# The first sorted expert blocks run between the last routing steps of chunks 2 and 3

## The reference

```python
# second layer: attention of the tokens to the context, then the experts
x = x + tanh(g_xattn[1]) * attend(layernorm(x), ctx)

xt = layernorm(x)                       # 2048 x 128
logits = xt @ Wr + br                   # 8 experts
pr, idx = top_k(logits, 2)
w = softmax(pr)                         # weights of the two chosen experts
for e in range(8):                      # DFF = 512
    h = silu(xt @ W1[e] + b1[e]) * (xt @ W2[e] + b2[e])
    y = y + (h @ W3[e] + b3[e]) * cw[:, e:e+1]
x = x + tanh(g_ffn[1]) * y
```

## Time and profile before

| | us |
|---|---|
| median of 3 runs | 659.05 |
| lowest and highest run | 655.75, 662.88 |
| the profiled execution's own time | 665.03 |
| its span, first to last instruction | 663.2 |
| outside the span in that execution | 1.8 |
| router logits of chunk 3 start (line 2071) | 512.94 |
| last row scatter of chunk 3 starts (line 776) | 529.30 |
| block 0's `up` starts; block 9's `up` starts (line 2156) | 520.05; 557.42 |

### The profile page before, as it was taken

The page is one execution under the profiler, slowest core; times in us unless marked ns, Lnnn a source line. Parts: engine busy times, 40 slices in busy tenths (PEclk is TensorE's granted clock), DMA queues, the critical chain, the costliest instruction groups (busy, mean ns, idle before and its releaser), DMA issues.

```text
span 663.2 us, 9902 instructions
## 1 busy us (share of the span) xinstructions
PE 569.0 (86%) x3306; PEld 341.7 (52%) x3318; DVE 430.7 (65%) x1054; ACT 307.7 (46%) x630; POOL 205.2 (31%) x214
## 2 busy tenths in 40 slices
PE   3777898988998699899999999998845579999993
PEld 1433444444443144344444445455635479999992
DVE  4898787887377879778334857768765444444454
ACT  2554364656667562455444435455332134444441
POOL 3829201010033686001750000012562723323330
PEclk9796798999998799899999999999795679999996
DMA  7694880000059100000021001000025158999965
GB/s 273 147 191 117 139 150 3 2 2 3 1 198 349 62 0 0 1 0 0 0 77 50 1 5 9 1 0 5 29 82 179 52 168 287 330 309 322 332 211 199
DMA packets 48198, 71.14 MB, mean 107 GB/s; under 512 B 11420, under 2 KB 35300, under 8 KB 47860
## 3 DMA queue, kind: packets, MB, share of 16 engines
q1 hardware_dynamic: 45156, 65.55, 34.3%
q0 software_dynamic: 2272, 4.69, 2.0%
q10 hardware_dynamic: 720, 0.27, 0.2%
HBM read 59.12 MB, written 21.29 MB: 121 GB/s over the span
## 4 chain that ended last, share of the span: by engine, by line
PE 42%; DVE 10%; issue 4%; DMA 4%; SPq 2%; POOL 2%; ACT 1%; another core or an unknown queue 1%; POOLq 0%; DVEq 0%
PE psum L1910 18%; PE psum L2156 6%; PE psum L2167 3%; DMA wb<-in_wall_dram 3%; PE psum L1839 3%; PE psum L1841 3%; PE psum L1907 2%; DVE hidden L1268 1%; PE psum L1989 1%; SPq L591 1%; DMA back<-sorted_y 1%; POOL sorted_x L776 1%; PE psum L1908 1%; PE psum L2017 1%
## 5 line engine op out<-in xcount | busy, mean ns | idle before, releaser
L1910 PE MATMUL psum<-hidden,ew 128*128 128x512 f32 x320 | 145.5, 598 | 0.6
L853 ACT ACTIVATE probs<-psum 128x512 f32<-128x512 f32 x128 | 72.7, 597 | 59.5 <-PE psum L1698 59.0
L1910 PEld LDWEIGHTS psum<-hidden,ew 128*128 128x128 f32 x320 | 61.3, 192 | 70.8 <-issue 69.6
L1127 DVE TENSOR_REDUCE negmax<-psum 128x4 f32<-128x1024 f32 x64 | 76.9, 1218 | 20.1 <-PE psum L1675 19.9
L1605 DVE SCALAR_TENSOR_TENSOR gated<-psum,wb,silu_g 128x128 f32<-128x128 f32 x156 | 43.8, 344 | 65.4 <-ACT silu_g L1047 50.0
L2156 PE MATMUL psum<-xbT,wb 128*128 128x128 f32 x624 | 80.5, 284 | 2.8 <-DMA wb<-in_wall_dram 2.5
L2156 PEld LDWEIGHTS psum<-xbT,wb 128*128 128x128 f32 x624 | 76.6, 200 | 4.0 <-DMA wb<-in_wall_dram 3.3
L1047 ACT ACTIVATE silu_g<-psum,wb 128x128 f32<-128x128 f32 x156 | 44.6, 369 | 69.6 <-PE psum L2156 49.0
L796 POOL DMA_INDIRECT sorted_y<-yb,xb x39 | 37.3, 956 | 80.4 <-DVE yb L1597 80.4
L1698 PE MATMUL psum<-stacks 50*128 50x256 bf16 x256 | 48.4, 289 | 9.8 <-ACT probs L853 4.3
L655 POOL TENSOR_SCALAR rstd<-meanvar 128x4 f32<-128x4 f32 x16 | 4.3, 270 | 158.2 <-DVE meanvar L1065 158.1
(11 more groups left out here) (253 smaller groups left out, 987.4 us busy)
## 6 DMA issues: line engine op xcount, KB each, us to landing
wb<-in_wall_dram SPq DMA_DIRECT2D x39, 516.0 KB
wb<-in_wall_dram SPq DMA_DIRECT2D x39, 256.0 KB
sorted_x<-in_slots_dram SPq DMA_DIRECT2D x1, 9815.0 KB, 32.6
stacks<-stacked SPq DMA_DIRECT2D x12, 384.0 KB, 9.1
xb<-sorted_x SPq DMA_DIRECT2D x39, 65.0 KB
stacked<-parts SPq DMA_DIRECT2D x6, 384.0 KB, 3.4
back<-sorted_y SPq DMA_DIRECT2D x4, 512.0 KB, 7.0
stacked<-parts SPq DMA_DIRECT2D x6, 256.0 KB, 3.3
```

The costliest lines, as they stand in the source:

```text
L853: nc.scalar.activation(probs[:, g % 2, h % 4, :, :], s2[n % 2].rearrange("p (k q) -> p k q", k=2), ACT.Exp, scale=float(HD) ** -0.5).then_ ...
L1127: nc.vector.tensor_reduce(negmax[:, p].rearrange("p h q -> p (h q)"), psum[:, i:i + 2, :].rearrange("p h (q k) -> p (h q) k", q=2), AX.X, ...
L1910: last = nc.tensor.matmul(dst, ew2[:, j, cols], hidden[:, c, k - 1, j, :], start=False, stop=(j == 3))
```

## The change

**Order on TensorE.** The transposes of blocks 0 to 4, `up` of blocks 0 to 2 and `down` of blocks 0 and 1 now stand among the routing steps of chunks 2 and 3. **Banks.** Blocks 0 to 8 (`j < EARLY`) share one set of four banks (3, 4, 5, 6); from block 9 on, odd blocks use banks 0, 1, 2, 7 and even ones 3, 4, 5, 6. Within the first nine blocks each step waits for the block just before it (`last_user`) to leave its bank. Chunk 3's transposes go to bank 0. **VectorE.** The products of blocks 0, 1 and 2 stand between `layer_norm_rows(3)`, `choose(3)`, `weights_of(3)` and `slots_of(3)`; the late table is written in three pieces behind blocks 3, 4 and 5; the shares behind block 12. **ScalarE.** The SiLU table is loaded ahead of the first blocks, the SiLUs of block 0 stand before chunk 3's copies, and `second_weights(2)` and `(3)` move to GpSimd as a power. **GpSimd.** Two of chunk 2's eight scatters now stand before `rstd_of_chunk(3, 3)`.

The diff, cut to its core:

```diff
-            return bank[(4, 5, 6, 6)[c]]
+            return bank[(4, 5, 6, 0)[c]]
+        def expert_bank(j, part):
+            i = ("up1", "up2", "down", "rows").index(part)
+            return bank[(0, 1, 2, 7)[i] if j >= EARLY and j % 2 else (3, 4, 5, 6)[i]]
+        def last_user(j):
+            return j - 1 if j < EARLY else j - 2
...
-            pool.wait_ge(gap2_ready, 1)
-            nc.gpsimd.tensor_tensor(w_top[:, 0:TC, 1], euler[:, 0:TC], gap2[:, 0:TC], ALU.pow).then_inc(w2nd_ready, 1)
+            def second_weights(c):
+                tc = slice(c * TC, (c + 1) * TC)
+                pool.wait_ge(gap2_ready, c + 1)
+                nc.gpsimd.tensor_tensor(w_top[:, tc, 1], euler[:, 0:TC], gap2[:, tc], ALU.pow).then_inc(w2nd_ready, 1)
+            second_weights(0)
             send_rows(0, range(0, 6))
...
             rstd_of_chunk(3, 2)
+            second_weights(2)
+            send_rows(2, range(0, 2))
             rstd_of_chunk(3, 3)
-            for c in range(EARLY_CHUNKS, NC):
-                send_rows(c, range(GR))
+            send_rows(2, range(2, GR))
+            second_weights(3)
+            send_rows(3, range(GR))
             for j in range(BLOCKS):
                 pool.wait_ge(yb_ready, j + 1)
...
             copy_probsT(7)
-            second_weights(2)
-            copy_xT3(3)
-            copy_rows(3)
-            second_weights(3)
             def copy_rowsT(j):
                 act.wait_ge(xbT_psum, j + 1)
                 if j >= 2:
                     act.wait_ge(up2_psum, j - 1)
-                nc.scalar.copy(xbT[:, j % 2, :], bank[6 + j % 2][:, 0:P]).then_inc(xbT_ready, 1)
-            copy_rowsT(0)
-            copy_rowsT(1)
-            for j in range(BLOCKS):
+                nc.scalar.copy(xbT[:, j % 2, :], expert_bank(j, "rows")[:, 0:P]).then_inc(xbT_ready, 1)
+            def silus(j):
                 act.wait_ge(up1_psum, j + 1)
                 if j >= 2:
                     act.wait_ge(gated_ready, MT * (j - 1))
                 for m in range(MT):
-                    nc.scalar.activation(silu_g[:, j % 2, m, :], bank[j % 2][:, m * P:(m + 1) * P], ACT.Silu,
+                    nc.scalar.activation(silu_g[:, j % 2, m, :], expert_bank(j, "up1")[:, m * P:(m + 1) * P], ACT.Silu,
                                          bias=wb[:, j % W_BUFS, B1_AT + m:B1_AT + m + 1]).then_inc(silu_done, 1)
+            nc.scalar.preload_act_table_set("silu_and_others")
+            copy_rowsT(0)
+            copy_rowsT(1)
+            silus(0)
+            copy_xT3(3)
+            copy_rows(3)
+            copy_rowsT(2)
+            for j in range(1, BLOCKS):
+                silus(j)
                 if j + 2 < BLOCKS:
                     copy_rowsT(j + 2)
...
+            gate_block(0)
+            choose(3)
+            gate_block(1)
+            keep_result(0)
+            weights_of(3)
+            gate_block(2)
+            keep_result(1)
+            slots_of(3)
+            for j in range(3, BLOCKS):
+                gate_block(j)
+                keep_result(j - 1)
+                if j == 3:
+                    late_counts()
+                if j == 4:
+                    late_jumps()
+                if j == 5:
+                    table_of(late_table, LATE, late_ready)
+                if j == EARLY + 3:
+                    dve.wait_ge(weighed, NC)
+                    steps.then(nc.vector.tensor_tensor(shares[:], is_top[:], xp[:, :, :, D + 1:ROW].to_broadcast([P, NT, 2, E]),
+                                                       ALU.mult))
+                    steps.wait()
+                    nc.vector.tensor_tensor(share[:], shares[:, :, 0, :], shares[:, :, 1, :], ALU.add).then_inc(share_ready, 1)
             keep_result(BLOCKS - 1)
             for c in range(NC):
...
+            def rows_T(j):
+                pe.wait_ge(xb_in[j % X_BUFS], 16 * (j // X_BUFS + 1))
+                if j == 0:
+                    pe.wait_ge(xT_ready, turn(3, 2))
+                elif j == EARLY:
+                    pe.wait_ge(counts_read, len(READS))
+                    pe.wait_ge(totals_read, len(TOTAL_OF))
+                else:
+                    pe.wait_ge(xbT_ready, last_user(j) + 1)
+                nc.tensor.transpose(expert_bank(j, "rows")[:, 0:P], xb[:, j % X_BUFS, 0:D], ident[:]).then_inc(xbT_psum, 1)
+            def up(j):
+                w = wb[:, j % W_BUFS, :]
+                pe.wait_ge(w_in[j % W_BUFS], 16 * (j // W_BUFS + 1))
+                pe.wait_ge(xbT_ready, j + 1)
+                if j == 0:
+                    pe.wait_ge(xT_ready, turn(2, 3))
+                    pe.wait_ge(x3_ready, B - 1)
+                if j == EARLY:
+                    pe.wait_ge(xT_ready, 4 * NC)
+                    pe.wait_ge(exp2_done, B)
+                for i, (part, psum, free) in enumerate((("up1", up1_psum, silu_done), ("up2", up2_psum, gated_ready))):
+                    if j and j != EARLY:
+                        pe.wait_ge(free, MT * (last_user(j) + 1))
+                    for m in range(MT):
+                        last = nc.tensor.matmul(expert_bank(j, part)[:, m * P:(m + 1) * P], w[:, i * FF + m * P:i * FF + (m + 1) * P],
+                                                xbT[:, j % 2, :], start=True, stop=True)
+                    last.then_inc(psum, 1)
+            def down(j):
+                w = wb[:, j % W_BUFS, W3_AT:W3_AT + MT * D]
+                pe.wait_ge(w3_in[j % W_BUFS], 16 * (j // W_BUFS + 1))
+                pe.wait_ge(gated_ready, MT * (j + 1))
+                if j == 0:
+                    pe.wait_ge(x3_ready, B)
+                elif j == EARLY:
+                    pe.wait_ge(probsT_ready, B)
+                else:
+                    pe.wait_ge(yb_ready, last_user(j) + 1)
+                for m in range(MT):
+                    last = nc.tensor.matmul(expert_bank(j, "down")[:, 0:D], gated[:, j % 2, m, :], w[:, m * D:(m + 1) * D],
+                                            start=(m == 0), stop=(m == MT - 1))
+                last.then_inc(down_psum, 1)
...
             route_logits(2)
             weigh_context(7)
+            rows_T(0)
             route_ranks(2)
+            rows_T(1)
+            up(0)
+            rows_T(2)
             rows_to_columns(3)
+            up(1)
+            rows_T(3)
             route_logits(3)
+            down(0)
+            up(2)
+            rows_T(4)
+            down(1)
             route_ranks(3)
-            pe.wait_ge(x3_ready, B)
-            pe.wait_ge(probsT_ready, B)
-            pe.wait_ge(xT_ready, 4 * NC)
-            pe.wait_ge(counts_read, len(READS))
-            pe.wait_ge(totals_read, len(TOTAL_OF))
...
+            for j in range(3, BLOCKS):
                 up(j)
                 if j + 2 < BLOCKS:
                     rows_T(j + 2)
-                if j:
-                    down(j - 1)
+                down(j - 1)
             down(BLOCKS - 1)
```

62 lines of the change are left out of this document (12 added, 50 removed).

## The result

| | us |
|---|---|
| changed kernel, median of 20 runs (lowest to highest) | 663.68 (659.21 to 670.00) |
| kernel before in the same comparison, median of 20 runs | 659.35 (655.75 to 672.16) |
| ratio to before, with its 95% interval | 1.0065 [1.0042, 1.0089] |
| the changed kernel's profiled execution; its span | 666.64; 664.7 |

The changed kernel is slower by 0.65%, some 4.3 us. That is within 1%, and inside the range of 650 to 666, but on the other side of "no change" from the forecast of 657.5. (The comparisons leave out executions in a disturbed state of the chip.)

A forecast was written before the change was run, and what follows sets the result against it. Block 9's start was taken to decide the time, held before by late blocks. Moving it from 557.42 to 550.4 took 7.0 us off the profiled 665.03, giving 658.0, shaded to 657.5 us; eight-in-ten range 650 to 666.

The forecast's parts named there:

- Steps 1 to 5: Chunk 3's path through its routing to its scatters: slots +10.6 us, last scatter +9.6 us (539.8), block 9 at 550.4.
- step 4: TensorE's early blocks and ranks before chunk 3's slots: ranks end at 529, slots ready at 529.9 against 519.26, +10.6 us.
- The clock rule: TensorE's clock is throttled by default and activity releases it; by that alone the sum would be about 654.
- Step 6: TensorE's blocks up to block 9: done at 545.7, 4.7 us to spare; late table near 540, early blocks' loads hidden.
- The sentence that the change is 3.1 us longer: Against an undisturbed kernel before, with block 9 at 547.3, the change was said to be 3.1 us longer.
- The second one: Rival: late signals on chunk 3's path or in the last scatters, holding block 5 and late table; 664 to 670; chance 0.17.
- its first half: Late signals of 6 to 9 us on chunk 3's path put block 9 at 557 to 560, time 664 to 667.
- The first rival: Full clock in the interleaved stretch, or late signals vanish: 654, or 650 with both; chance of under 652.5: 0.25.

The follow-up runs named there:

- routing_first: The changed kernel with chunk 3's routing ahead of blocks 1 and 2, deviation ahead of the scatters, late table in one piece: 658.43 us, ratio 0.9967 to before.
- table_at_once: The changed kernel with the late table written in one piece right behind chunk 3's slots: 661.51 us over six runs, no ratio given.
- after_spaced_third: The changed kernel with a GpSimd power behind every second scatter of chunks 2 and 3 and every third writeback of blocks 0 to 8: ratio 0.9997.
- deviation_first: The changed kernel with GpSimd's deviation for chunk 3 ahead of all of chunk 2's scatters again: 661.62 us, ratio 0.9979 to before.
- spaced_scatters: The kernel before with a GpSimd power of 128x4 behind every second scatter of chunks 1, 2 and 3: 660.32 us, ratio 0.9998.
- after_again: The changed kernel without edit, on another chip beside the kernel before: 666.11 us, ratio 1.0045.
- after_spaced: The changed kernel with a GpSimd power behind every second scatter of chunks 2 and 3 and each writeback of blocks 0 to 8: 662.30 us, ratio 1.0019.

## Why the prediction was wrong

*Steps 1 to 5, right, and 2 us too dear.* Chunk 3's slots came 8.6 us later than before, at +66.2, where step 4 had +10.6 or 529.9 - 461.49 = +68.4; the last scatter ended at +76.5 for +78.3; `up(3)` started at +65.4 for +67.5. Of the 2 us, 0.9 were there when the normalisation began (+51.3 for +52.2), for which the sum had no term. The clock gave 1.8, as logits and `down(0)` ran in 0.96 and 1.14 us where I took 1.88 and 2.05 from rows at half clock; and part of that was lost again, since `up(2)`'s second half waited 2.48 us for the products of block 1. routing_first shows that the whole delay comes from this order.

*The clock rule.* From 501 to 508.5 TensorE was busy 7.41 of 7.5 us at a granted clock of 0.50. During `up(0)`, from 508.5 to 511.3, the mean was 0.75, and it took 2.67 us (1.95 at full clock, 3.75 at half). Then TensorE idled 5.4 us; from 516.7 to 517.8 the clock was 0.50 again, `up(1)` took 3.15 us, and from 520.7 to 522.7, with the logits and `down(0)`, it was 1.00. The sum by the Trainium skill's rule (TensorE: Matmul & The Clock Gate, "Part 1: The HAM clock gate"), that activity releases the clock, had `up(1)` at full clock. The trace agrees with the rule in so far as the clock rose during `up(0)` and during `up(1)`, but not with that sum, which left out the idle time between them; and the busy stretch ahead of `up(0)` at half clock speaks against the rule for the work that stands there.

*Step 6, the step that failed.* It put late signals in the changed kernel at nothing. It gave TensorE 4.7 us to spare, the late table near 540 and the loads of the early blocks "hidden", and the sum took the 10 us of late signals out of the recorded execution as a gain that the change brings. Two things were wrong in it. The late signals did not go with the order of the blocks; they go with GpSimd's run of indirect DMAs, and with the end of that run they moved from blocks 0 and 1 to blocks 3 to 5. TensorE was ready for block 9 at about +94.5 where step 6 had 545.7 - 461.49 = +84.2, so 10.3 us late, more than twice the 4.7 to spare. And they held the late table (+87.0 in place of +78.5) and the third weights of block 7 in SyncE's queue, behind which the rows of block 9 stand; the queue alone still holds them when the table comes early (table_at_once). Block 9 stood at +95.1 where 550.4 - 461.49 = +88.9 was forecast, 6.2 us later. With the signals on time it stood at +89.5 (after_spaced_third), 0.6 us from the sum for an *undisturbed* changed kernel. Part of that agreement is luck: chunk 3's slots were some 2.5 us earlier than forecast there (+65.8), its scatters, with spacers, took 13.2 us where the forecast had 9.8, and block 9 came 10.0 us behind them, not 10.6.

The other error is the baseline. I knew that the profiled execution lay 6.0 us above the median, and still took the gain off its time and gave the result as the changed kernel's median. The sentence that the change is 3.1 us longer against an undisturbed kernel before was the better forecast: measured 4.4 us (1 to 8) with the signals spaced in both kernels, and 4.3 us as they are. With the signals on time TensorE waits 5.31 us for rows that hang on the scatters (after_spaced_third), so early blocks done ahead of time buy nothing there; what the change pays is 8.6 us of chunk 3's way to these scatters. How much of the 4.3 us comes by that way in an ordinary execution the profiles do not show; that the loss goes when chunk 3's routing goes first (1.0065 and 1.0045 to 0.9967) is the evidence for it.

*The rivals.* The second one named late signals in the last scatters that hold block 5 and the late table, worth up to 3 us more; this half of it came, and cost more than that (block 9 6.2 us later), though by TensorE's own blocks as much as by the table, while its first half, on the path of chunk 3, did not, and showed only in deviation_first. Its guess that the lateness may be work and not a signal does not fit these blocks: later matmuls of the same engine had recorded starts, at their usual distance, while the signal was out. Whether the writing of the results to PSUM or the signal behind it is late, starts alone do not tell. The first rival had the clock half right (`up(1)` 3.15 us, not 1.95) and the end of late signals wrong.

*Still open.* Why chunk 0's slots stand anywhere between 457 and 471 us in programs whose work is the same up to there. How long GpSimd's pause must be, and what in it lets the signals through; and how long a run must be to delay them, since six scatters in the changed kernel went without a late signal and six writebacks in spaced_scatters did not. And how often executions of the kernel before that were not profiled hold late signals; that spacing scatters and writebacks takes 0.7 to 1.1% off it suggests that many do. after_again and after_spaced differ less than their intervals, so what late signals cost the changed kernel's median is known only from its profiles.

## What to carry to other kernels

Before you call a wait a gain, find out what makes it: one that ends with "remote" while the engine that should signal has long begun its next work does not go away when the waiting work is moved; it strikes whatever waits then. Work that fills an idle stretch is free only if it stands *behind* the chain that ends the stretch in every engine's order; here the same blocks ahead of the last chunk's routing gave a ratio of 1.0065, behind it 0.9967 (not yet told from 1), and with spaced scatters 0.9881. And make the sum against a kernel without its disturbance on both sides, not against one profile that holds it.

## What the runs showed of the hardware

In these traces TensorE's signals arrive late when GpSimd issues many indirect DMAs without a pause (0.96 us each, 1.26 us apart). In the changed kernel eleven in a row (530.65 to 544.34) went with waits of 4.01, 5.43 and 5.84 us that ended with "remote"; with a power of 1.04 us behind every second scatter of chunks 2 and 3 and every third writeback no wait ended so in that place, in three different kernels; with a memset of 0.12 us they stayed, at 8.7 and 9.0 us. Short runs did no harm: six scatters (515.48 to 522.96) had no wait that ended with "remote" beside them, nor had the three writebacks in a row of the last kernels. TensorE went on to later blocks until it needed an answer, and then idled (3.08 and 2.64 us), with the clock at 0.50 from 541.8 to 548.6. What carries the signals was not measured.
